# Graph network layer on one core: the dense follow-up of a 512-node chunk moved two steps later on TensorE and ScalarE, and the last two chunks interleaved

## What is computed

```python
h = relu(layernorm(x))
feat_all = einsum('ni,rhid->rnhd', h, conv_weights)     # 8 relations x 4 heads x 64
el, er   = scores of source and target per edge
alpha    = softmax over the edges of one target of leaky_relu(el + er)
x = x + segment_sum(alpha * feat_src, dst) + h_bias     # x1: end of the attention layer
h = relu(layernorm(x))
h = h @ W_in + b_in                                     # input layer of the second network
for l in range(3):
    agg = segment_sum(h[src], dst) / deg
    h = relu(agg @ W_agg[l] + h @ W_self[l] + b_hid[l])
x = x + h @ W_out + b_out
```

## Time and profile before

| | us |
|---|---|
| median of 3 runs | 2599.94 |
| the three runs | 2577.82 to 2600.36 |
| the profiled execution | 2594.63 |
| its span (first to last instruction) | 2592.7 |
| walk, from the first gather to POOL's last | 609.6 to 1433.0 |
| step 41's group sum kept, ACT L1144 | 1461.72 |
| last rows stored, SP L1596 | 1514.23 |
| third part's first load, SP L1795 | 1526.93 |
| busy: PE, DVE, ACT, POOL (share of the span) | 84%, 54%, 28%, 23% |

### The profile page before, as it was taken

The page is one execution under the profiler, slowest core; times in us unless marked ns, Lnnn a source line. Parts: engine busy times, 40 slices in busy tenths (PEclk is TensorE's granted clock), DMA queues, the critical chain, the costliest instruction groups (busy, mean ns, idle before and its releaser), DMA issues. The chain is left out here.

```text
span 2592.7 us, 29932 instructions
## 1 busy us (share of the span) xinstructions
PE 2173.1 (84%) x9258; PEld 1197.8 (46%) x9259; DVE 1387.6 (54%) x3828; ACT 718.1 (28%) x2133; POOL 584.9 (23%) x549
## 2 busy tenths in 40 slices
PE   2389999995777786778776749999989999999999
PEld 1243334333555464556554424444544444544445
DVE  5779999994456564555565528878821111101001
ACT  0134444442445453445444521010000001000000
POOL 3200000004776665757575100000000000000000
PEclk7589999997776787877777879999989999999999
DMA  5024444445444443535353323222222222233432
GB/s 148 15 97 147 154 148 154 157 154 173 125 126 129 124 140 99 150 103 156 109 152 109 69 89 102 92 82 82 71 83 90 82 86 87 82 115 98 124 98 81
DMA packets 249540, 290.31 MB, mean 112 GB/s; under 512 B 53330, under 2 KB 212247, under 8 KB 249111
## 3 DMA queue, kind: packets, MB, share of 16 engines
q1 hardware_dynamic: 195278, 181.12, 22.8%
q0 software_dynamic: 24192, 67.12, 9.9%
q10 hardware_dynamic: 29896, 39.99, 4.4%
HBM read 201.20 MB, written 86.96 MB: 111 GB/s over the span
## 5 line engine op out<-in xcount | busy, mean ns | idle before, releaser
L1905 PE MATMUL PS<-a_sb,y_sb 128*128 128x512 f16 (+2 forms) x4320 | 874.3, 363 | 43.5 <-DVE y_sb L1981 30.9
L1070 POOL DMA_INDIRECT work<-feat_tab,fidx_i x504 | 543.9, 1079 | 791.3 <-issue 653.1
L1905 PEld LDWEIGHTS PS<-a_sb,y_sb 128*128 128x128 bf16 (+1 forms) x4320 | 407.9, 98 | 509.7 <-issue 69.7
L1275 PE MATMUL PS<-work,stg 128*128 128x260 f32 x1008 | 328.4, 483 | 3.2 <-issue 2.4
L1130 ACT ACTIVATE work<-work 128x64 f32<-128x64 f32 x1344 | 327.3, 332 | 7.5 <-issue 7.1
L233 DVE TENSOR_SCALAR side<-iota_c,col_t 128x512 f16<-128x512 f16 x940 | 329.0, 350 | 0.2
L243 PE MATMUL PS<-side 128*128 128x512 f16 x940 | 254.2, 383 | 20.2 <-DVE side L233 12.4
L1275 PEld LDWEIGHTS PS<-work,stg 128*128 128x128 f32 x1008 | 231.7, 242 | 71.1 <-issue 24.6
L1995 DVE TENSOR_TENSOR mean<-PS,rdeg 128x1024 f32<-128x1024 f32 (+1 forms) x24 | 27.2, 1134 | 416.0 <-PE PS L1905 415.7
L1847 ACT ACTIVATE hT<-mean,bh_c 128x512 f32<-128x512 f32 (+1 forms) x48 | 30.3, 678 | 789.4 <-DVE mean L1999 789.4
L232 DVE TENSOR_SCALAR side<-iota_c,rel 128x128 f16<-128x128 f16 x940 | 236.4, 251 | 0.2 <-PE PS L243 0.2
(11 more groups left out here) (243 smaller groups left out, 1637.0 us busy)
## 6 DMA issues: line engine op xcount, KB each, us to landing
a_sb<-a_tab SPq DMA_DIRECT2D x126, 640.0 KB, 4.3
feat_tab<-stg ACTq DMA_DIRECT2D x120, 260.0 KB, 2.1
a_tab<-side SPq DMA_DIRECT2D x235, 128.0 KB, 1.7
stg<-dst_tab SPq DMA_DIRECT2D x42, 384.0 KB
work<-feat_tab,fidx_i POOLq DMA_INDIRECT x504
h_tab<-outs SPq DMA_DIRECT2D x42, 130.0 KB
h_tab<-outs SPq DMA_DIRECT2D x8, 520.0 KB, 3.2
stg<-h_tab SPq DMA_DIRECT2D x8, 520.0 KB
```

Source lines behind the costliest of these rows:

```text
L1070: pool.indirect_dma_start(out=ring[:, s, 0:FE], out_offset=None, in_=feat_tab[:, :], in_offset=bass.IndirectOffsetOnAxis(ap=idx, axis=0)). ...
L1275: mm = pe.matmul(PS[:, OUTS[j], 0:EXT], onehot[:, t, :], ring[:, j * U + t, 0:EXT], start=(t == 0), stop=(t == U - 1), skip_group_check=True)
L1905: mm = pe.matmul(SUMS(ug, n)[:, f, :], y_sb[l % 2][0:rows_of, kb, s, f * P:(f + 1) * P], a_sb[0:rows_of, load % SLOTS, kb % KB, 0:n], star ...
```

## The change

`part` is split. `ready(c)`, DVE's part and ACT's square root, stays at the end of step `CHUNK_END[c]` + 1. `rows(c)`, the rows on PE and ACT, now stands at the end of step `CHUNK_END[c]` + 3, for the same chunk c, and no longer beside a chunk's `ready`. So the rows of chunks 0 to 5 lie within the walk, and those of 6 and 7 behind it. There they are interleaved, and chunk 7 (`LATE`) has its own banks (0 and 1) and its own buffers for `hn`, the relu's result and the rows. `h0` now also holds the stored rows in place of `mid`, so the wait for the store moves from L1165 to L1174's copies. SP stores y one step after x, together with the reload of x.

```diff
-        BOUND = PS[:, 5:7, :]
+        BANKS = [PS[:, 5:7, :], PS[:, 0:2, :]]
+        LATE = NC - 1
+        late = lambda d: 1 if d == LATE else 0
+        turned_in, kept_in = [mid, side[:, 0:1024]], [h0, stg[:, 1536:2560]]
+        hn = [b4(hn_b), b4(side[:, 1024:2048])]
...
-        def walk(eng, step, part, begin):
+        def walk(eng, step, begin, ready, rows, tail):
...
                     step(s // G, s % G, last=(s == SUBS - 1))
                     if s - 1 in CHUNK_END:
-                        part(CHUNK_END.index(s - 1))
-                part(NC - 1)
-                part(NC)
+                        ready(CHUNK_END.index(s - 1))
+                    if s - 3 in CHUNK_END:
+                        rows(CHUNK_END.index(s - 3))
+                tail()
...
-                def part(c):
-                    first = c == 0
-                    if not first:
-                        turned(c - 1)
-                    if c < NC:
-                        root(c)
-                    if not first:
-                        rest(c - 1)
+                def rows(d):
+                    turned(d)
+                    inner(d)
+                    outer(d)
+
+                def tail():
+                    turned(LATE - 1)
+                    root(LATE)
+                    inner(LATE - 1)
+                    turned(LATE)
+                    outer(LATE - 1)
+                    inner(LATE)
+                    outer(LATE)
...
-                walk(act, step, part, begin)
+                walk(act, step, begin, root, rows, tail)
...
+                def tail():
+                    turn(LATE - 1)
+                    inner(LATE - 1)
+                    turn(LATE)
+                    outer(LATE - 1)
+                    inner(LATE)
+                    outer(LATE)
...
-                walk(pe, step, part, begin)
+                walk(pe, step, begin, lambda c: None, rows, tail)
...
-                    wait_past(dve, s_t2, c)
-                    ln_finish(dve, rows, c, 0, s_sd2, s_rs2, s_hn, hn)
+                    if c < LATE:
+                        wait_past(dve, s_t2, c)
+                    ln_finish(dve, rows, c, 0, s_sd2, s_rs2, s_hn, hn[late(c)])
...
                         if s - 3 in CHUNK_END:
-                            store_part(CHUNK_END.index(s - 3))
+                            store_x(CHUNK_END.index(s - 3))
                         if s - 4 in CHUNK_END:
+                            store_y(CHUNK_END.index(s - 4))
                             reload(CHUNK_END.index(s - 4))
```

## The result

The changed kernel took 2627.58 us in the median of 4 runs (2626.84 to 2634.47), the kernel before 2599.06 us in 4 (2577.82 to 2600.36). The ratio is 1.0135, with a 95% interval from 1.008 to 1.019. Forecast were 2588 us, and 2566 to 2626.

A forecast was written before the change was run, and what follows sets the result against it. POOL's gathers and its stops for PE bound the walk; +5.2 us there (82.2 for 77.0) and -17 in the tail gave -11.8, so a median of 2588 us, 8 in 10 within 2566 to 2626.

The forecast's parts named there:

- Step (1): Sign in the profile: twelve long POOL waits on PE in turns, six near 6.6 us and six near 10.5.
- A: Rival, chance 0.24: stalls in the walk add up, rows cost full 14.1 us each; 2620 in all; break-even 15.7 a chunk.
- DVE's part alone, 4.9 us: Walk, six places behind `ready`: each costs POOL 4.9 us as part 0 did, 29.4 in all.
- step (2): Sign: from `keep` to the next scan about 11.7 us behind `ready` and 17 behind `rows`.
- Rows alone, 14.1 us late: Walk, six places: rows make steps 14.1 us late and cost 8.8 each after absorption, 52.8 in all.
- The 5.3 us absorbed: Walk: POOL's ring of three steps absorbs 5.3 us of each rows stall, as in a double part (19.7 - 14.4).
- The tail, -17 us: Behind the last step: last copy at 1496.9 in place of 1514.2, with chunks 6 and 7 interleaved; bounds -22 to -12.
- step (3): Sign in the tail: ACT's last copy 35 us after step 41's `keep`, not 52.5.
- B: Rival, chance 0.14: DVE's part costs nothing in five of six places of the walk; -36 in all, 2564 us.
- D: Rival, chance 0.10: the tail shortens by only 5 us, x and y waiting for the same queue; 2600.
- C, the clock: Rival, chance 0.10: after five more idle stretches PE runs the next step at lower clock; +12 in all, 2612.
- The exponential's table: Rows alone in the walk: its 1.28 us load need not recur in the next step, so 15.4 becomes 14.1.

The follow-up runs named there:

- walk alone: The changed kernel with the last two chunks one after the other in one set of banks and buffers: 0.9987 of before at 2463 us, 1.0133 at 2600.
- thirds: The changed kernel with each chunk's rows cut in three successive steps (transposes, input layer, output layer), y stored two steps later: 0.9842 of before at 2600 us.
- halves: The kernel with rows cut over three steps, with DVE's normalization and bias also moved one step behind its statistics: 0.9714 of before, 0.9727 when run again.
- tail alone: The changed kernel with the walk's order of before (rows beside the next chunk's DVE part): 0.9960 of before at 2463 us, 0.9926 at 2600.

## Why the prediction was wrong

- **The frame was right.** POOL's stops set the walk, and the change makes twelve of them in place of six, in turns. Step (1) of "What would show it" told the cases apart: near 10.5 us for the rows by the forecast, near 16 under A, 17.0 measured.
- **DVE's part alone, 4.9 us.** It was mis-sized a little: 5.4 to 6.8 by the run without it. In the first profile the stops average 7.0, less the ordinary 1.7, so 5.3; in the second 8.4, so 6.7. From `keep` to the scan it is 11.5 to 11.7 us in five of six, as step (2) said, and 13.0 in one.
- **Rows alone, 14.1 us late: this step failed.** Its first half, from relu to the scan, was sized right: 13.0 to 15.9, mean 13.9. What failed is the rest, "PE waiting ahead of its transposes" for loads, of which the prediction says "That wait moves to `ready`". It did not move. Behind `keep` the copy comes after 15.6, 9.2, 8.8, 10.2, 8.5 and 4.2 us, mean 9.4, as in the double parts of before (8.9). From `keep` to the scan that makes 23.3 in the mean where I had 17, so the rows come 23.3 - 2.8 = 20.5 late and not 14.1.
- **The 5.3 us absorbed** held in the sum's own terms: the stops are 17.0 - 1.7 = 15.3 beyond the ordinary, 5.2 less than the 20.5. What it means is different, though. The 7 to 8 us that POOL still issues behind `keep` cover the wait for the copy, and nothing is left for the 13.9 us of the rows. The error of the sum is 6 x (15.3 - 8.8) = 39 us for the rows and 2 for DVE's part, less 1 in the tail; the result was 39.6 above the forecast. The signs were there. In the earlier trace rows relu's wait is marked "remote", not as one for a load. And the ordinary step of the earlier trace rows, 2.8 us, was a short one: the ordinary steps of before average 5.2 from `keep` to the scan and take up to 15.6, so every "late" of the prediction is counted from too low a base. Why the results are held is open.
- **Why the double parts were cheap.** A double part of before takes 22.6 us from `keep` to the scan and stops POOL for 16.1 in the mean; rows alone take 23.3 and 17.0. So DVE's part ran for nothing within the time that the held results and the rows took anyway. Whoever takes it out of that cover pays for it in full, and the rows get nothing for it. At 2600 us a chunk then costs 13.5 to 14.9 + 5.4 to 6.8 = 18.9 to 21.7 us, where before paid 77.0 / 6 = 12.8. Both are beyond the break-even of 15.7 that stood under A. The sum with the measured mean, 6 x 20.3 = 121.8, is 44.8 above 77.0; with the tail's 18.0 that is +26.8, where 28.5 was measured.
- **The tail, -17 us.** The rows of the changed kernel behind its last step that answer to the earlier trace rows, `keep`, chunk 7's root, the two outer layers and the last copy:

```profile
1518.25 0.39 ACT L1151 ACTIVATE outs<-PS 128x260 f32<-128x260 f32 x1 [2.70 <-PE PS L1309]
...
1530.96 0.30 ACT L1175 ACTIVATE std<-mv,eps_c 128x4 f32<-128x4 f32 x1 [4.33 <-DVE mv L821]
...
1535.96 3.72 PE L1339 MATMUL PS<-wbuf,stg 128*128 128x256 f32 x16 [1.64 <-ACT hT L1185]
...
1545.62 5.41 PE L1339 MATMUL PS<-wbuf,stg 128*128 128x256 f32 x16 [2.51 <-ACT hT L1185]
1551.07 1.02 ACT L1190 ACTIVATE stg<-PS 128x1024 f32<-128x1024 f32 x1 [5.50 <-PE PS L1339]
```

  The root waits for DVE alone, and the last copy ends 33.8 us behind `keep`; step (3) said 35. The gain is -18.6 against the first profile of before, -18.0 against the second. The size was right. The reason was only half right: walk alone, without the turns, has nearly the same tail, since the block of rows has left it.
- **A**, at 0.24, named the direction and nearly the price (2620, and 14.1 us a chunk for the rows where 15.3 was measured), but by luck. Its mechanism was that DVE's stop two steps earlier leaves no time to gain a new one. The run without DVE's part has no such stop, and the rows stop POOL for 17.8 us all the same. The lead was there and went into the wait ahead of the rows. **B** is excluded by the run without DVE's part. **D** is excluded by the tail.
- **C, the clock.** In windows of the changed kernel (us, then PE, PEld, DVE, ACT and POOL busy, PE's granted clock, DMA share, GB/s) behind a stop for DVE's part, and behind one for rows:

```profile
1062.00:1080.00 18.00, 10.44 (x59) 7.65 (x58) 7.05 (x22) 10.13 (x36) 11.74 (x12) 0.87 0.42 123
1113.00:1127.00 14.00, 11.85 (x66) 8.64 (x64) 11.57 (x30) 10.31 (x45) 11.26 (x10) 1.00 0.58 152
```

  The clock is at 0.87 and 1.00 of full speed there, so mostly at 2.4 GHz. From the scan to the next `keep` it averages 0.84 in the six steps behind DVE's part and 0.78 in the ordinary ones, so C did not happen. Where the clock does show is within the rows, from relu to the scan (chunks 2 and 3):

```profile
1097.70:1110.80 13.10, 9.52 (x26) 5.57 (x27) 0.00 (x0) 3.51 (x6) 0.00 (x0) 0.81 0.01 3
1225.30:1241.20 15.90, 12.29 (x26) 7.06 (x27) 0.01 (x1) 3.57 (x6) 0.00 (x0) 0.67 0.01 1
```

  The four blocks at 0.80 to 0.81 take 13.0 to 13.2 us, the two at 0.67 to 0.69 take 15.0 and 15.9.
- **The exponential's table.** It was put at the wrong place. Its load comes behind the scan and behind the gather that ends the stop, so it shortens no stop, and the 14.1 should have been 15.4. What it costs there the exponentials show, of before (scan at 911.69 in the earlier trace rows) and of the change (scan at 1110.83 above):

```profile
921.38 0.21 ACT L1122 ACTIVATE work<-PS 128x48 f32<-128x48 f32 x1
```

```profile
1119.24 0.21 ACT L1129 ACTIVATE work<-PS 128x48 f32<-128x48 f32 x1 [3.69 <-issue]
```

  They start 9.69 and 8.41 us behind the scan, 1.28 apart, and the same in all five double parts and all six blocks of rows to 0.02 us. The Trainium skill, "ScalarE: Activation LUTs", section "What ACT_TABLE_LOAD costs", has 2.66 us for a switch; here only the load's 1.28 stands on the path.
- **The likeliest case's own range.** The bounds that it names (tail -22 to -12, 8 us of queue) give 2583 to 2601, not 2576 to 2603. The result lies outside either.

## What to carry to other kernels

A buffer's lead can be spent only once. Here a wait ahead of the extra work had used it up, and the work itself was paid in full; so look at what the producer (POOL) does at the moment the extra work starts, and not only at how long the work is. Two pieces of work that stand together may share one stop, and taking them apart saves nothing if the longer one keeps the whole stop. If they must be moved, cut them so small that each piece fits into one step's slack, with the engines' halves in different steps: thirds gave 0.984 and halves besides 0.971, with the same arithmetic.

## What was not expected of the hardware

- PE's increments reach the others late while the gathers run: 6.3 us in the median behind L1241 in the changed kernel, up to 22 us, and released 1.2 to 2.6 us after POOL's last gather in 15 of the 18 blocks of rows of the change's two profiles and the walk alone. The cause is open, and which of the two follows from the other is not shown: no run spaced the gathers out. The sums have a part in it: with one of the twelve the delay is 2.2 us in the median, and results given out ahead of all twelve were not held in four of six chunks.
- The same kernel took 2463 us on one chip, 5% less than on the others. The profiles taken there have a delay of 0.01 us in every step. The tail alone was profiled on both sides, 2441.4 and 2576.2 us, and 132.4 of the 134.8 us between them lie between the first gather and step 41's `keep`. On that chip the walk's new order cost 5 to 10 us where it cost over 50 on the others (tail alone against walk alone). What differs between the chips is not known, and a verdict on such a change holds for the condition in which it was measured.
